# Message stages by pairs of groups, and a node stage with its closing additions on POOL, in a graph network kernel on one core

## The reference

```
h = relu(layernorm(x));  loops = arange(N)            # block 1: four attention layers
for i in range(4):
    fs = (h @ W[i]).reshape(N, 4, 64)
    e = leaky_relu((fs * al).sum(-1)[src_e] + (fs * ar).sum(-1)[dst_e], 0.2)
    alpha = softmax of e over the edges with one destination
    h = segment_sum(alpha * fs[src_e], dst_e) + b, summed over the 4 heads
x = x + h + h_bias
h = relu(layernorm(x))                                # block 2: a gated convolution
t = batch_norm(concat(h[src], h[dst], edge_attr) @ W_full + b_full)
upd = segment_sum(sigmoid(t[:, :64]) * softplus(t[:, 64:]), dst)
x = x + softplus(h + batch_norm(upd))
```

## Time and profile before

| | us |
|---|---|
| median of 3 runs | 3288.08 (3281.88 to 3289.84) |
| the profiled execution | 3270.75 |
| its span | 3268.0 |
| PE busy, of the span | 2087.7 (64%) |
| DVE busy | 2035.8 (62%) |
| POOL busy | 1800.3 (55%) |
| ACT busy | 1147.7 (35%) |

### The profile page before, as it was taken

How to read it: one execution, slowest core, us unless ns; L and a number is a source line. 1 busy time by engine, 2 the same in 40 slices (tenths; PEclk the granted TensorE clock), 3 DMA queues, 4 the chain that set the end, 5 groups by cost and what they waited for, 6 DMA issues and landing times. The chain is left out here.

```text
span 3268.0 us, 39692 instructions
## 1 busy us (share of the span) xinstructions
PE 2087.7 (64%) x11638; PEld 1539.0 (47%) x11638; DVE 2035.8 (62%) x3688; ACT 1147.7 (35%) x2352; POOL 1800.3 (55%) x1700
## 2 busy tenths in 40 slices
PE   1434444458958867957877967786968888111386
PEld 0333333346735545735645745554745555000285
DVE  3544445477746648746647746657956667766598
ACT  0222222234422213412313422212324455665386
POOL 5555555535655553655663655563765553577433
PEclk9656555569966658966667966656987889555698
DMA  2333333331124410124420124431322222222375
GB/s 49 80 82 87 85 84 82 86 87 39 63 69 103 106 36 30 60 64 101 112 55 22 60 56 105 103 70 26 106 74 60 62 63 53 51 68 73 103 237 170
DMA packets 336365, 255.35 MB, mean 78 GB/s; under 512 B 175756, under 2 KB 284617, under 8 KB 336132
## 3 DMA queue, kind: packets, MB, share of 16 engines
q1 hardware_dynamic: 287876, 202.20, 20.9%
q0 software_dynamic: 43904, 48.80, 7.9%
q10 hardware_dynamic: 4372, 1.82, 0.2%
HBM read 132.21 MB, written 124.48 MB: 79 GB/s over the span
## 5 line engine op out<-in xcount | busy, mean ns | idle before, releaser
L1104 POOL DMA_INDIRECT edge<-table,row_of_source x588 | 560.3, 953 | 416.7 <-DVE h_new L1190 190.0
L935 POOL TENSOR_TENSOR scaled<-edge 128x512 f32<-128x512 f32 x196 | 336.6, 1718 | 272.9 <-PEq L1025 146.0
L989 DVE TENSOR_TENSOR_SCAN wide<-keep,wide,banks 64x256 f32<-64x256 uint8 x392 | 291.8, 744 | 123.7 <-PE banks L1042 111.1
L208 POOL DMA_INDIRECT edge<-in_x_dram,src_row x196 | 191.7, 978 | 228.0 <-DMA x_dst<-got 153.0
L1012 ACT ACTIVATE scaled_t<-banks 128x1024 f32<-128x1024 f32 x196 | 200.8, 1024 | 308.6 <-PE banks L1034 308.6
L1145 PE MATMUL banks<-wide,w_row 128*64 128x512 f32 x294 | 260.2, 986 | 53.5 <-DVE h_new L1190 42.7
L1152 PEld LDWEIGHTS banks<-w_edge_full,wide 128*128 128x128 f32 x1176 | 228.4, 289 | 110.1 <-issue 96.5
L1584 POOL DMA_INDIRECT node_rows<-rows_conv,scatter_row x196 | 200.2, 1022 | 134.2 <-issue 68.0
L1332 POOL DMA_INDIRECT edge<-table,row_of_x x196 | 194.1, 990 | 136.5 <-DVE h_new_last L1429 72.3
L1167 PE MATMUL banks<-w_node,n_norm_t 65*128 65x64 f32 x784 | 157.9, 368 | 174.2 <-issue 98.5
L1152 PE MATMUL banks<-w_edge_full,wide 128*128 128x72 f32 x1176 | 235.6, 370 | 43.8 <-DVE self_logit L1200 42.8
(11 more groups left out here) (299 smaller groups left out, 4561.1 us busy)
## 6 DMA issues: line engine op xcount, KB each, us to landing
node_rows<-x_out SPq DMA_DIRECT2D x97, 256.0 KB
wide<-node_rows SPq DMA_DIRECT2D x48, 512.0 KB, 3.8
table<-chain_rows SPq DMA_DIRECT2D x147, 136.0 KB
table<-rows SPq DMA_DIRECT2D x147, 136.0 KB, 2.3
nodes<-in_x_dram SPq DMA_DIRECT2D x97, 128.0 KB
table<-x_out SPq DMA_DIRECT2D x97, 128.0 KB
out_dram<-n_soft SPq DMA_DIRECT2D x48, 256.0 KB, 2.2
sources<-src_pad SPq DMA_DIRECT2D x49, 196.0 KB
```

The costliest lines, as they stand in the source:

```text
L208: pool.indirect_dma_start(out=to, out_offset=None, in_=x, in_offset=bass.IndirectOffsetOnAxis(ap=rows[:, tile:tile + 1], axis=0),).then_in ...
L935: pool.tensor_tensor(scaled[:, s, SHARE:], edge[:, mine, 0:D].unsqueeze(2).broadcast_to([P, TPG - SHARE, H, D]), inner(edge[:, mine, D:ROW ...
L989: v.tensor_tensor_scan(out=wide[0:D, bass.ds(first + 1, HALF_E)], data0=keep[:, s, half * HALF_E:(half + 1) * HALF_E], data1=bank[2 + s][h ...
L1104: pool.indirect_dma_start(out=edge[:, at_tile], out_offset=None, in_=tables[l], in_offset=bass.IndirectOffsetOnAxis(ap=row_of_source[:, at ...
```

## The change

In `messages` for l = 0 to 2 the groups go by turns of two, `[0, 1], [2, 3], ... [46, 47], [48]`. In a turn each engine does one kind of work for both groups before the next kind. For l = 3 the order is as before. Two waits of PE go for all four layers: they are implied by others.

In the node stage DVE's `finish` is gone. POOL adds the argument to x instead (`add_argument`, step i-5) and adds the logarithm to that (`add_log`, step i-6). The last store, of 106 partitions, is split into one of 96 and one of 10. The block no longer makes POOL drain at its end.

```
+                turns = [[k, k + 1] for k in range(0, G - 1, 2)] + [[G - 1]]
+                def in_turns(fn, ks):
+                    for k in ks:
+                        fn(k, k, k % 2, k // 2)
 # SP, l < 3
+                        for i, ks in enumerate(turns):
+                            in_turns(load, ks)
+                            if i > 0:
+                                in_turns(save, turns[i - 1])
+                        in_turns(save, turns[-1])
 # DVE, l < 3
+                        in_turns(scale, turns[0])
+                        for i, ks in enumerate(turns):
+                            if i + 1 < len(turns):
+                                in_turns(scale, turns[i + 1])
+                            in_turns(scan, ks)
 # ACT, l < 3
+                        for i, ks in enumerate(turns):
+                            in_turns(take, ks)
+                            if i > 0:
+                                in_turns(stage, turns[i - 1])
+                        in_turns(stage, turns[-1])
 # PE: in transpose, and in message
-                        t_.wait_ge(taken, at(k, back=2))
-                        t_.wait_ge(summed, at(k, back=2))
 # PE, l < 3
+                        for i, ks in enumerate(turns):
+                            in_turns(transpose, ks)
+                            if i > 0:
+                                in_turns(next_rows, turns[i - 1])
+                            in_turns(message, ks)
+                        in_turns(next_rows, turns[-1])
 # node stage
-            block = st.enter_context(nc.Block())
+            block = st.enter_context(nc.Block(no_gpsimd_drain=True))
+                    first, rest = slice(0, used // 16 * 16), slice(used // 16 * 16, used)
+                    sp.dma_start(to[first], n_soft[first, s % OUT_SLOTS]).then_inc(stored[s % OUT_SLOTS], 16)
+                    if used % 16:
+                        sp.dma_start(to[rest], n_soft[rest, s % OUT_SLOTS]).then_inc(stored[s % OUT_SLOTS], 16)
-                def finish(k, g, s, turn):
-                    v.wait_ge(n_logged, at(k))
-                    v.tensor_tensor(n_soft[:, s % OUT_SLOTS], n_norm[:, s % OUT_SLOTS], n_soft[:, s % OUT_SLOTS], ALU.add).then_inc(n_whole, 1)
-                pipelined(v, ((5, normalize), (5, argument), (2, take2), (4, variance), (6, finish)), lead=LEAD, slots=SLOTS)
+                pipelined(v, ((5, normalize), (5, argument), (2, take2), (4, variance)), lead=LEAD, slots=SLOTS)
-                def add_x1(k, g, s, turn):
-                    pool.wait_ge(n_whole, at(k))
-                    pool.tensor_tensor(n_soft[:, s % OUT_SLOTS], n_soft[:, s % OUT_SLOTS], nodes[:, s, :, 0:D], ALU.add).then_inc(n_ready, 1)
-                pipelined(pool, ((6, add_x1),), lead=LEAD, slots=SLOTS)
+                def add_argument(k, g, s, turn):
+                    pool.wait_ge(n_arg, at(k))
+                    pool.tensor_tensor(nodes[:, s, :, 0:D], nodes[:, s, :, 0:D], n_norm[:, s % OUT_SLOTS], ALU.add).then_inc(n_based, 1)
+                def add_log(k, g, s, turn):
+                    pool.wait_ge(n_based, at(k))
+                    pool.wait_ge(n_logged, at(k))
+                    pool.tensor_tensor(n_soft[:, s % OUT_SLOTS], n_soft[:, s % OUT_SLOTS], nodes[:, s, :, 0:D], ALU.add).then_inc(n_ready, 1)
+                pipelined(pool, ((6, add_log), (5, add_argument)), lead=LEAD, slots=SLOTS)
```

More of the change, by code:

```diff
@@ L924, in messages @@
                 SHARE = 2
+                turns = [[k, k + 1] for k in range(0, G - 1, 2)] + [[G - 1]]
+                assert sum(turns, []) == list(range(G))
+                def in_turns(fn, ks):
+                    for k in ks:
+                        fn(k, k, k % 2, k // 2)
                 @block.gpsimd
@@ L965, in _ @@
                         sp.sem_inc(saved[s], 32)
-                    pipelined(sp, ((1, load), (1, load_x), (5, save)), lead=5)
+                    if last_step:
+                        pipelined(sp, ((1, load), (1, load_x), (5, save)), lead=5)
+                    else:
+                        for i, ks in enumerate(turns):
[3 more added lines that the diff above has]
+                        in_turns(save, turns[-1])
                     sp.wait_ge(saved[0], 16 * (G // 2 + 1) + 32)
@@ L1000, in _ @@
                     v.memset(wide[0:D, 0:1], 0.0).then_inc(sp_paced, 1)
-                    pipelined(v, ((0, scale), (3, scan)) + (((5, stage),) if last_step else ()), lead=5)
+                    if last_step:
+                        pipelined(v, ((0, scale), (3, scan), (5, stage)), lead=5)
+                    else:
+                        in_turns(scale, turns[0])
[3 more added lines that the diff above has]
+                            in_turns(scan, ks)
                 @block.scalar
@@ L1018, in stage @@
                         s_.activation(rows[:, s], bank[4 + s][:, 0:TPG * width].rearrange("p (t w) -> p t w", w=width), ACT.Copy).then_inc(rows_ready, 1)
-                    pipelined(s_, ((1, take),) + (() if last_step else ((4, stage),)), lead=5)
+                    if last_step:
+                        pipelined(s_, ((1, take),), lead=5)
+                    else:
+                        for i, ks in enumerate(turns):
[3 more added lines that the diff above has]
+                        in_turns(stage, turns[-1])
                 @block.tensor
@@ L1052, in next_rows @@
                         last.then_inc(rows_in_psum, 1)
-                    pipelined(t_, ((1, transpose), (4, next_rows), (2, message)), lead=5)
+                    if last_step:
+                        pipelined(t_, ((1, transpose), (4, next_rows), (2, message)), lead=5)
+                    else:
+                        for i, ks in enumerate(turns):
[4 more added lines that the diff above has]
+                        in_turns(next_rows, turns[-1])
         def spread(l):
@@ L1721, in build @@
             n_in_psum, n_taken, n_taken2, n_out, n_squared, n_summed2, n_log, n_rstd, n_normed, n_arg, n_exped, n_logged, \
-                n_whole, n_ready = [
+                n_based, n_ready = [
                     sem(st, f"{name}_out") for name in (
                         "n_in_psum", "n_taken", "n_taken2", "n_out", "n_squared", "n_summed2", "n_log", "n_rstd", "n_normed",
-                        "n_arg", "n_exped", "n_logged", "n_whole", "n_ready")]
+                        "n_arg", "n_exped", "n_logged", "n_based", "n_ready")]
             sp_paced = sem(st, "sp_paced_out")
             pe_paced = sem(st, "pe_paced_out")
-            block = st.enter_context(nc.Block())
+            block = st.enter_context(nc.Block(no_gpsimd_drain=True))
             made = lambda k: banks[:, 2 * (k % 3) + 2:2 * (k % 3) + 4].rearrange("p b (t w) -> p b t w", w=2 * D)
@@ L1743, in save @@
                     sp.sem_inc(sp_paced, 1)
-                    sp.dma_start(out[bass.ds(k * GN, used * NODE_T)].rearrange("(p j) f -> p j f", j=NODE_T), n_soft[0:used, s % OUT_SLOTS]).then_inc(stored[s % OUT_SLOTS], 16)
+                    to = out[bass.ds(k * GN, used * NODE_T)].rearrange("(p j) f -> p j f", j=NODE_T)
+                    first, rest = slice(0, used // 16 * 16), slice(used // 16 * 16, used)
+                    sp.dma_start(to[first], n_soft[first, s % OUT_SLOTS]).then_inc(stored[s % OUT_SLOTS], 16)
+                    if used % 16:
+                        sp.dma_start(to[rest], n_soft[rest, s % OUT_SLOTS]).then_inc(stored[s % OUT_SLOTS], 16)
                 for s in range(OUT_SLOTS):
@@ L1749, in _ @@
                 for s in range(OUT_SLOTS):
-                    sp.wait_ge(stored[s], 16 * uses[s] + 16)
+                    sp.wait_ge(stored[s], 16 * uses[s] + (32 if s == (G - 1) % OUT_SLOTS and LAST_P % 16 else 16))
             @block.tensor
@@ L1778, in _ @@
             def _(v):
-                for signal in (n_taken2, n_summed2, n_normed, n_arg, n_whole):
+                for signal in (n_taken2, n_summed2, n_normed, n_arg):
                     v.sem_inc(signal, AHEAD)
@@ L1810, in _ @@
                 pool.sem_inc(n_ready, SLOTS)
-                def add_x1(k, g, s, turn):
-                    pool.wait_ge(n_whole, at(k))
+                pool.sem_inc(n_based, AHEAD)
+                def add_argument(k, g, s, turn):
[4 more added lines that the diff above has]
+                    pool.wait_ge(n_logged, at(k))
                     pool.tensor_tensor(n_soft[:, s % OUT_SLOTS], n_soft[:, s % OUT_SLOTS], nodes[:, s, :, 0:D], ALU.add).then_inc(n_ready, 1)
-                pipelined(pool, ((6, add_x1),), lead=LEAD, slots=SLOTS)
+                pipelined(pool, ((6, add_log), (5, add_argument)), lead=LEAD, slots=SLOTS)
             @block.scalar
```

## The result

The changed kernel takes 3268.42 us (median of 6 runs, 3264.74 to 3276.76), the kernel before 3289.89 (6 runs, 3281.88 to 3294.85): a ratio of 0.994, with a 95% interval of 0.9922 to 0.9959. That is 21.5 us less, and the forecast of 3268.9 holds.

A forecast was written before the change was run, and what follows sets the result against it. It took PE to bound the message stages and the loop variance, rstd, normalize the node stage. Terms 12.9 + 2.2 + 0.1 + 3.95 + 0.1 = 19.2 us off 3288.08 gave 3268.9, range 3258 to 3281.

The forecast's parts named there:

- A turn of two groups: Message stages, PE: one of two round trips between column widths goes, so a turn falls from 5.76 to 5.505 us.
- Rival 1: Message stages: the passage between column widths isn't the cost, a turn stays at 5.76 us; 3285.6 in all, 7%.
- rival 2: Message stages: R1 waits for its scan, each of 66 turns 0.2 us longer than 5.505; 3282 in all, 8%.
- Start and end of a stage: Message stages: 1.8 us lost at the start, 0.47 less at the end; one stage gives 4.3 us, three 12.9.
- Rival 3: Message stages: DVE and POOL collide over their scales, DVE's taking up to 1.53 us instead of 0.66; 3311 in all, 6%.
- The node stage's steps: Node stage: full steps stay at 3.34 us without finish, a gain of 0 us in some 45 steps.
- Rival 4: Node stage: DVE bounds it after all, steps fall towards 3.0 us, 13.5 us more gained; 3255 in all, 5%.
- one of two loops: Node stage: variance, rstd, normalize and on to the next variance add up to the whole period, 3.34 us.
- The last load: End of the node stage: the last group's load starts 2.2 us earlier, PE waits 3.0 us in place of 5.2.
- the lower clock: End of the node stage: PE's T took 1.94 us against 1.09 after the wait; a shorter wait might spare 1.3 more.
- the last addition: End of the node stage: finish goes but POOL has three additions in a row; 0.1 us taken, bounds 0 and 1.2.
- The last store and the drain: End of the kernel: the split store lands after 2.6 us instead of 6.5, 3.95 us gained; the drain gives 0.1.

The follow-up runs named there:

- r5: The changed kernel with PE's turn in the order T0, R0, T1, R1, M0, M1; a turn took 5.53 us.
- r6: The changed kernel with PE's turn in the order T0, T1, R0, M0, R1, M1; a turn took 5.80 us.
- r7_split_store: The kernel before with the last store in two transfers, POOL's drain kept; the span ended 7.1 us after the issue, as before.
- r9: The changed kernel with normalize, argument, softplus and POOL's two additions one step later, four buffers for n_logs; full node-stage steps averaged 3.02 us.
- r11: The kernel before without POOL's drain at the end, the last store whole; last store's issue to the span's end 7.0 us.

## Why the prediction was right, point by point

**A turn of two groups.** Predicted 5.505, measured 5.51; T(4) to T(48) predicted at about 121, measured 879.30 - 758.06 = 121.24. The cause, passages between M and the 128-column products, is shown by the pair r5 and r6. Rival 1 falls, and rival 2: PE never waits for a scan in a full turn.

**Start and end of a stage.** T(0) to T(4) grew by 1.96 where 1.8 was predicted, and T(48) to R(48) fell by 0.33 (6.35 after, 6.68 before) where 0.47 was predicted. With 5.48 for the full turns a stage gives 5.48 - 1.96 + 0.33 = 3.85, not 4.3; three give 11.5, not 12.9. The mechanism was right. Start and end were mis-sized by 0.3 together, and the full turns gave 5.48 in place of 5.61, since a turn is 5.511 and not 5.505.

**Rival 3, the collision of the scales.** POOL's second scale was issued before DVE's two, and took 2.41 us, while DVE's two took 1.26 together, 0.63 each:

```profile
842.90 2.41 POOL L944 TENSOR_TENSOR scaled<-edge 128x512 f32<-128x512 f32 x1
```

It is POOL that gives way, in time that it has. By the rule of the Trainium skill weighed there ("SBUF — State Buffer", Who interferes with whom: the first to issue holds the shared port) DVE would have waited; in the full turns the measurement decides against it, as the row of before did. It is not so everywhere: in the first 6 us of the stage, in both kernels, the DVE scales took 1.36 to 1.53, beside POOL scales that started before them. What decides between the two cases stays open.

**The node stage's steps.** Predicted unchanged at 3.34, and they are, to 0.01; DVE stands 0.61 before normalize, as announced. Rival 4, the reading of DVE's gapless rows as a bound, falls. The prediction knew one of two loops; the second lay, by the estimate above, 0.18 lower and decided nothing here.

**The last load.** It was issued 2.1 us earlier against T(47), where 2.2 was predicted. PE's step from T(47) to T(48) was 8.0 to 8.2 us in the five executions with the node stage of before and 5.0 to 6.4 in the five with the changed one, 2.5 less in the mean. Whether the shorter wait spares the lower clock, which the prediction valued at 1.3 and left out of its sum, differs from one execution to the next. In the changed kernel's profile it didn't: T ran at the full clock (1.07 us after, 1.94 before), but then the granted clock was 0.5 (1.2 GHz) from about 3249 to 3252, under the products of `rows`, and T(48) to the end of the last addition took 15.7 us as before. In `r5_trtrmm` and `r6_ttrmrm`, with the same node stage and waits of 2.2 and 2.6 us, it stayed at 1.0 (2.4 GHz), and that stretch took 14.3. The products in the changed kernel and in `r5_trtrmm`:

```profile
3248.62 5.37 PE L1813 MATMUL banks<-center_mat,nodes_t 128*128 128x128 f32 x32
```

```profile
3248.18 3.74 PE L1814 MATMUL banks<-center_mat,nodes_t 128*128 128x128 f32 x32
```

Over the five executions of each node stage the stretch took 15.7 to 16.9 before and 14.3 to 15.9 after, 1.4 less in the mean. The 0.1 predicted for the last addition can't be told apart in that.

**The last store and the drain.** Predicted 3.95 + 0.1, measured 4.2. The sum is right and its split is wrong: I gave the drain 0.1 and the store all the rest, but with the drain kept the store alone gives 0. The step that failed is "The drain can give at most the 0.5 between landing and the span's end", read from a wait that ended 0.3 before POOL's drain, of which the prediction has no row. The rule of the Trainium skill against splitting a transfer by partitions into halves ("DMA: Bandwidth & Descriptors", Rules for kernel authors) does not carry over to 106 partitions split into 96 and 10. The rule on the number of engines (same page, "Why a DMA increments its semaphore by 16 and not by 1") does hold: while the whole store ran (3262 to 3267 in the kernel before) the mean busy share of the 16 DMA engines was 0.13, which is 2 of 16, and while the two parts ran (3281.2 to 3282.5 in `r7_split_store`) it was 0.53.

**The sum.** The stages give 11.5 for the pairs and 8.1 for the node stage, 19.6 us, where 19.2 were predicted; the medians differ by 21.5 in one set of runs and 15.5 in the other, both within their uncertainty of it. That the terms agree so well in the sum is partly luck: the pairs gave 1.4 less than predicted, and the node stage 1.7 more, most of it in the stretch behind T(48), for which the sum had 0.1. Luck too is that the median came within 0.5 us of the forecast; the changed kernel's other set has a median of 3276.76. And the forecast for the profiled execution, 3251.5, missed: it took 3268.28. The prediction carried over the distance of 17.3 us between the profiled execution and the median as if it belonged to the kernel, but by the table above that execution had a low draw of the stages that gather rows.

## What to carry to other kernels

A gapless engine is not yet the bound: follow its operation's inputs round through the other engines, add up every loop and divide by the steps it spans; what is taken off an engine inside a loop's shadow gives nothing, and giving the loops one more step of lag took a tenth off the stage's full steps here. Products of different kinds should be done in batches, if buffers allow. Where two things end together at the end of a program, remove both or neither, and test them singly: SP's waits named only the store here, and the chain only POOL.

## What the runs showed of the hardware

- A passage between T or R (128 weight columns) and M (64 weight columns, in pairs) cost about 0.135 us, though no row shows PE idle.
- POOL's drain at the end of the last block took 8.25 us, of which 7.0 after its last addition, with the store whole (landed 0.3 before its end) and split (4.3 before it).
- A transfer of 106 partitions landed in 6.5 us (store, 212 KB) and 10.8 to 12.2 (load, 424 KB); in 96 and 10 it was under 3, and under 5.1. During the whole store the mean busy share of the 16 DMA engines was 0.13.
- The stages that gather rows took 322 to 338 us on the first chips and 248 on the chip of r9 to r11, where the kernel before ran in 2741 instead of 3290, with the message and node stages of that kernel the same to 1 us (147.6 to 148.6 and 193.5 in `r11_no_drain`). On POOL's gathers (L1104) the first line below is the profile of before, the second `r11_no_drain`; what made DVE late on the slower chips was not looked into, and stays open.

```profile
  DVE h_new L1190: 190.0, 55
```

```profile
  DVE h_new L1190: 2.7, 9
```
